# Layer 1's first head in a four-layer cross-attention kernel: its weights split in layer 0's attention, its keys formed in layer 0's FFN

## The reference

```python
# layer 0, FFN: the router picks 2 of 8 experts, but only experts 0 and 1 exist
weights = softmax(tokens @ gate_w); topk_w, topk_idx = top_k(weights, 2)
e0 = silu(x @ w0.T + b0); e1 = silu(x @ w1.T + b1)
out = e0 * fw[:, 0:1] * (fidx[:, 0:1] == 0) + e1 * fw[:, 1:2] * (fidx[:, 1:2] == 1)
# layer 1, attention: 8 heads of 128 over all 896 tokens and all 3000 keys
qh, kh, vh = split_heads(x @ Wq), split_heads(context @ Wk), split_heads(context @ Wv)
sim = einsum('hid,hjd->hij', qh, kh) * SCALE; mean = sim.mean(-1, keepdims=True)
attn = softmax((sim - mean) * 1.5 + mean)
out = merge_heads(einsum('hij,hjd->hid', attn, vh)) @ Wout + bout
# layer 1, FFN: weights rounded to -1, 0, 1 times their mean absolute value
scale = 1.0 / clip(mean(abs(w)), 1e-05); wq = clip(round(w * scale), -1, 1) / scale
```

## Time and profile before

| | |
|---|---|
| median of three executions | 1935.88 us |
| the profiled execution, its own time | 1937.66 us |
| its span from first to last instruction | 1935.7 us |
| TensorE busy, products | 1793.0 us, 93% |
| VectorE busy | 1410.4 us, 73% |
| ScalarE busy | 1020.4 us, 53% |
| GpSimd busy | 507.4 us, 26% |

### The profile page before, as it was taken

The page is one execution under the profiler, slowest core; times in us unless marked ns, Lnnn a source line. Parts: engine busy times, 40 slices in busy tenths (PEclk is TensorE's granted clock), DMA queues, the critical chain, the costliest instruction groups (busy, mean ns, idle before and its releaser), DMA issues. The chain is left out here.

```text
span 1935.7 us, 33792 instructions
## 1 busy us (share of the span) xinstructions
PE 1793.0 (93%) x11747; PEld 1585.4 (82%) x11750; DVE 1410.4 (73%) x3157; ACT 1020.4 (53%) x2247; POOL 507.4 (26%) x531
## 2 busy tenths in 40 slices
PE   7958999999999999999967999999969999999698
PEld 6637999999898989899845888888857888888587
DVE  6478787777777787778666566666777777777786
ACT  4344656555556555565535565556622666666421
POOL 0514030211203030302011233333441444343342
PEclk9978999999999999999988999999989999999799
DMA  4011000000000000000021112110000000000011
GB/s 160 1 77 33 2 4 9 2 10 0 11 0 11 0 12 0 3 0 1 1 98 49 53 58 64 47 64 14 9 1 17 15 9 23 9 10 4 23 56 40
DMA packets 17591, 48.43 MB, mean 25 GB/s; under 512 B 2602, under 2 KB 7347, under 8 KB 15796
## 3 DMA queue, kind: packets, MB, share of 16 engines
q1 hardware_dynamic: 16596, 45.99, 7.3%
q10 hardware_dynamic: 864, 0.83, 0.1%
HBM read 45.89 MB, written 0.92 MB: 24 GB/s over the span
## 5 line engine op out<-in xcount | busy, mean ns | idle before, releaser
L1280 ACT ACTIVATE a_pH<-banks 125x512 fp32r<-125x512 f32 (+1 forms) x384 | 203.9, 544 | 273.6 <-PE banks L195 192.2
L1351 DVE TENSOR_TENSOR a_pL<-banks,a_pH 125x512 fp32r<-125x512 f32 (+1 forms) x384 | 235.2, 623 | 100.3 <-ACT a_pH L1280 96.6
L1854 POOL TENSOR_TENSOR a_prob<-a_prob,a_rinv 112x750 f32<-112x750 f32 x128 | 184.1, 1438 | 395.9 <-DVE a_rinv L2157 395.9
L1327 DVE TENSOR_SCALAR_CACHE_REDUCE a_prob<-banks 128x500 f32<-128x500 f32 x336 | 223.1, 677 | 18.0 <-PE banks L195 9.0
L1181 PE MATMUL banks<-ident,a_prob 128*125 128x128 f32 x1344 | 201.6, 274 | 6.6 <-ACT a_prob L1265 4.4
L195 PE MATMUL banks<-a_pH,a_head_vH 125*128 125x256 f32 (+1 forms) x576 | 203.2, 353 | 2.1 <-DVE a_pL L1351 1.1
L1265 ACT ACTIVATE a_prob<-a_prob,a_nmax 128x1000 f32<-128x1000 f32 x168 | 188.0, 1122 | 28.2 <-DVE a_nmax L1330 28.2
L1181 PEld LDWEIGHTS banks<-ident,a_prob 128*125 128x125 f32 x1344 | 187.1, 188 | 10.0 <-ACT a_prob L1265 4.9
L1137 POOL TENSOR_TENSOR a_head_oH<-a_o,ones 128x256 fp32r<-128x256 f32 (+1 forms) x24 | 16.5, 687 | 625.5 <-DVE a_o L1360 625.5
L195 PE MATMUL banks<-a_pH,a_head_vL 125*128 125x256 f32 (+1 forms) x576 | 173.0, 300 | 0.0
L195 PE MATMUL banks<-a_pL,a_head_vH 125*128 125x256 f32 (+1 forms) x576 | 172.8, 300 | 0.0
(11 more groups left out here) (422 smaller groups left out, 5094.9 us busy)
## 6 DMA issues: line engine op xcount, KB each, us to landing
a_w_out<-in_f_out SPq DMA_DIRECT2D x6, 1024.0 KB, 4.8
...
```

Of the source, the lines that this page charges most:

```text
L1280: act.activation(pH[:, c % RING, 0:wide], TB[c % 4][0:KB, 0:wide], ACT.Copy).then_inc(t_high, 1)
L1327: dve.tensor_scalar(prob[:, at, c * CHUNK:(c + 1) * CHUNK], SB[c % 3][:, 0:CHUNK], SCALE, None, ALU.mult, ALU.max, accum_out=chunk_max[:, ...
L1351: dve.tensor_tensor(pL[:, c % RING, 0:wide], TB[c % 4][0:KB, 0:wide], pH[:, c % RING, 0:wide].bitcast(F32), ALU.subtract).then_inc(t_done, 1)
L1854: pool.tensor_tensor(both, both, rinv[:, n % RING, :].unsqueeze(2).to_broadcast([SEQ, 2, KEYS]), ALU.mult).then_inc(p_normed, 1)
```

## The change

Nine things are done in one change.

1. `PairWeights` is allocated ahead of layer 0, and layer 1's heads use its buffers. One buffer `raw` holds the pair's raw weights, or a head's (`head_raw`), or layer 0's key and value weights, which lie there first.
2. In layer 0's attention SyncE loads head 0's weights of layer 1 into it once layer 0's have been split, and GpSimd splits them (`first_head_cut`) after the context.
3. Keys of layer 1's head 0 (`s.kH`, `s.kL`) are formed in layer 0's FFN, in banks 0 to 2: chunks 0 to 2 on TensorE at the start of the phase, chunks 3 to 5 behind tiles 3 to 5 of the expert loop.
4. In that FFN GpSimd waits until x is normed before it splits the expert weights; the high part is formed by ScalarE, ahead of the turn of x. The first of the three `quant_raw` loads moves ahead of the expert weights, and its sum of absolute values ahead of the turn.
5. The other two sums stand behind the SiLUs of tiles 0 and 2. `QUANT_AT` goes from 2 to 3; the last rounding and all three conversions stand behind the loop.
6. The bias comes as 128 rows of which only rows 0 and 64 are not zero; the high part fills rows 0 to 63 and the low part rows 64 to 127, and one product with a square of ones adds both. It is 256 KB then.
7. Expert tile 0 is formed between the router's products and the transposes of the logits.
8. In layer 1 head 0 begins with four units of values, then transposes, queries, scores of tiles 0 and 1, then the other eight units. The first query waits for the bank of value unit 0, the second for that of unit 1. GpSimd adds the bias to x ahead of splitting the output weights, and head 1's weights are loaded at the start.
9. The helpers are cut up so that one unit can be issued by itself (`value_unit`, `query_half`, `key_terms`, `high_value_unit`, `sum_value_unit`, `low_query_half`). In the loop over heads they issue the same instructions as before, but the low part of the queries is a subtraction without a factor of 1.0.

```diff
-        wkv = sb("a0_wkv", [P, 2, 2, D])
+        wkv = s.pair.raw[:].rearrange("p (w k d) -> p w k d", w=2, k=2)
...
+            sp.wait_ge(w_cut, 1)
+            sp.dma_start(s.pair.head_raw, dram["a1_w"][0]).then_inc(head_loaded, 16)
...
+            pool.wait_ge(cut_done, 3 * PIECES)
+            first_head_cut(pool, s.pair, head_loaded, head_high, head_cut)
...
+    if between is not None:
+        between()
...
-        QUANT_AT = 2
+        QUANT_AT = 3
+        KEYS_AHEAD = 3
+        KEYS_BEHIND = (3, 4, 5)
+        ABS_BEHIND = (0, 2)
...
-        one = sb("f0_one", [1, P], F32R)
+        bias = sb("f0_bias", [P, WIDE])
+        bias_both = sb("f0_bias_both", [P, WIDE], F32R)
+        one = sb("f0_one", [P, P], F32R)
...
-        EB = B[4:8]
+        EB = [B[6], B[7], B[4], B[5]]
+        KEY_BANKS = B[0:3]
...
+            sp.dma_start(quant_raw[:, 0, :], dram["f1_w"][:, 0, :]).then_inc(quant_loaded[0], 16)
-            sp.dma_start(bias[:], dram["f0_bias"]).then_inc(w_loaded, 16)
-            for m in range(3):
+            sp.dma_start(bias[:], dram["f0_bias"]).then_inc(bias_loaded, 16)
+            for m in range(1, 3):
...
-            pool.tensor_copy(one[:], s.ones[0:1, :])
-            pool.wait_ge(w_loaded, 32)
-            pool.tensor_copy(biasH[:], bias[:]).then_inc(bias_high, 1)
-            pool.tensor_copy(wH[:], w_raw[:]).then_inc(w_cut, 1)
+            pool.tensor_copy(one[:], s.ones[:])
+            pool.wait_ge(ql.normed, TILES)
+            pool.wait_ge(w_high, 1)
+            pool.tensor_tensor(wL[:], w_raw[:], wH[:].bitcast(F32), ALU.subtract).then_inc(w_cut, 1)
+            pool.wait_ge(bias_loaded, 16)
+            pool.tensor_copy(bias_both[:], bias[:]).then_inc(bias_high, 1)
             pool.wait_ge(bias_high, 1)
-            pool.tensor_tensor(biasL[:], bias[:], biasH[:].bitcast(F32), ALU.subtract)
-            pool.wait_ge(w_cut, 1)
-            pool.tensor_tensor(wL[:], w_raw[:], wH[:].bitcast(F32), ALU.subtract).then_inc(w_cut, 1)
+            pool.tensor_tensor(bias_both[P // 2:P, :], bias[P // 2:P, :], bias_both[P // 2:P, :].bitcast(F32),
+                               ALU.subtract).then_inc(bias_cut, 1)
...
+            def key_low(c):
+                dve.wait_ge(k_high, c + 1)
+                dve.tensor_tensor(s.kL[:, key_cols(c)], KEY_BANKS[c % 3][:, 0:CHUNK], s.kH[:, key_cols(c)].bitcast(F32),
+                                  ALU.subtract).then_inc(k_low, 1)
...
+            for c in range(KEYS_AHEAD):
+                key_low(c)
+            at = router_exps(dve, r, q, B[3])
...
+                if i in KEYS_BEHIND:
+                    key_low(KEYS_AHEAD + KEYS_BEHIND.index(i))
+            for m in range(TILES - QUANT_AT - 2, 3):
+                quant_round(dve, m)
...
+            load_table(act, s, ACT.Sqrt)
+            key_high(0)
             layer_norm_scalar(act, ln, ql)
+            abs_sums(0)
+            act.wait_ge(w_loaded, 16)
+            act.activation(wH[:], w_raw[:], ACT.Copy).then_inc(w_high, 1)
             turn_scalar(act, ql, B[4:8], s.xnTH)
+            for c in range(1, KEYS_AHEAD):
+                key_high(c)
             router_scalar(act, r, q, B[4:8])
...
-                if i < 3:
-                    act.wait_ge(quant_loaded[i], 16)
-                    need(act, abs_summed, i)
-                    act.activation(abs_out[:], quant_raw[:, i, :], ACT.Abs, accum_out=abs_sum[:, i:i + 1]).then_inc(abs_summed, 1)
                 act.wait_ge(e_filled, i + 1)
                 need(act, x_added, i - POST + 1)
                 act.activation(post[:, i % POST, :], EB[i % 4][:, :], ACT.Silu).then_inc(post_ready, 1)
-                if i >= QUANT_AT + 3:
-                    brought_back(i - QUANT_AT - 3)
-            for m in range(TILES - QUANT_AT - 3, 3):
+                if i in ABS_BEHIND:
+                    abs_sums(1 + ABS_BEHIND.index(i))
+                if i in KEYS_BEHIND:
+                    key_high(KEYS_AHEAD + KEYS_BEHIND.index(i))
+            for m in range(3):
...
-            turn_and_route(pe, s, ql, xn, B[4:8], r, q, B[0])
+            def keys(c):
+                need(pe, k_low, c - 2)
+                split_products(pe, KEY_BANKS[c % 3][:, 0:CHUNK], key_terms(s.pair.wH, s.pair.wL, s, c)).then_inc(k_filled, 1)
+
+            def expert(i):
                 tok = slice(i * P, (i + 1) * P)
                 need(pe, post_ready, i - 3)
                 split_products(pe, EB[i % 4][:, :], [
                     pair for k in range(KT) for pair in (
                         (s.xnTH[:, k, tok], wH[:, k, :]), (s.xnTH[:, k, tok], wL[:, k, :]),
-                        (s.xnTL[:, k, tok], wH[:, k, :]))]
-                    + [(one[:], biasH[:]), (one[:], biasL[:])]).then_inc(e_filled, 1)
+                        (s.xnTL[:, k, tok], wH[:, k, :]))], True, False)
+                if i == 0:
+                    pe.wait_ge(bias_cut, 1)
+                pe.matmul(EB[i % 4][:, :], one[:], bias_both[:], start=False, stop=True).then_inc(e_filled, 1)
+
+            def first_expert():
+                pe.wait_ge(w_cut, 1)
+                expert(0)
+
+            for c in range(KEYS_AHEAD):
+                keys(c)
+            turn_and_route(pe, s, ql, xn, B[4:8], r, q, B[3], first_expert)
+            for i in range(1, TILES):
+                if i == QUANT_AT + 2:
+                    pe.wait_ge(abs_summed, 3)
+                    pe.wait_ge(q.step, 1)
+                    pe.matmul(B[3][:, 0:3], s.ones[:], abs_sum[:], start=True, stop=True).then_inc(abs_total, 1)
+                expert(i)
+                if i in KEYS_BEHIND:
+                    keys(KEYS_AHEAD + KEYS_BEHIND.index(i))
...
+        self.w_raw, self.wH, self.wL, self.wv = s.pair.head_raw, s.pair.wH, s.pair.wL, s.pair.head_wv
+        self.kH, self.kL = s.kH, s.kL
...
-    sp.dma_start(w.w_raw[:], dram_w[0]).then_inc(q.loaded, 16)
     sp.dma_start(w.wo_raw[:], dram_wo[0]).then_inc(q.wo_loaded, 16)
-    with sp.Fori(1, HEADS) as h:
-        sp.wait_ge(q.wv_cut, h)
-        sp.wait_ge(q.qk_cut, h)
+    sp.dma_start(w.w_raw[:], dram_w[1]).then_inc(q.loaded, 16)
+    sp.wait_ge(q.wo_cut, 1)
+    sp.dma_start(w.wo_raw[:], dram_wo[1]).then_inc(q.wo_loaded, 16)
+    with sp.Fori(2, HEADS) as h:
+        sp.wait_ge(q.wv_cut, h - 1)
+        sp.wait_ge(q.qk_cut, h - 1)
...
+def first_head_cut(pool, w, loaded, high, cut):
+
+    pool.wait_ge(loaded, 16)
+    pool.tensor_copy(w.wH[:], w.head_raw[:, 0:4, :]).then_inc(high, 1)
+    pool.tensor_copy(w.head_wv[:, :, 0, :], w.head_raw[:, 4:6, :]).then_inc(high, 1)
+    pool.wait_ge(high, 2)
+    pool.tensor_tensor(w.wL[:], w.head_raw[:, 0:4, :], w.wH[:].bitcast(F32), ALU.subtract).then_inc(cut, 1)
+    pool.tensor_tensor(w.head_wv[:, :, 1, :], w.head_raw[:, 4:6, :], w.head_wv[:, :, 0, :].bitcast(F32),
+                       ALU.subtract).then_inc(cut, 1)
...
-            return 0 if isinstance(h, int) and h == 0 else EACH * h - GROUPS
+            return EACH * h - GROUPS - CHUNKS
+
+        FIRST_FILLED = [("v", 0), ("v", 1), ("v", 2), ("v", 3), ("q", 0), ("q", 1)] + [("v", n) for n in range(4, VUSES)]
+        FIRST_DONE = [("v", 0), ("v", 1), ("q", 0), ("q", 1)] + [("v", n) for n in range(2, VUSES)]
+        first_filled = {each: n + 1 for n, each in enumerate(FIRST_FILLED)}
+        first_done = {each: n + 1 for n, each in enumerate(FIRST_DONE)}
+        first_bank = {each: TB[n % 4] for n, each in enumerate(FIRST_FILLED)}
+        last_in_bank = {each: FIRST_FILLED[n - 4] for n, each in enumerate(FIRST_FILLED) if n >= 4}
...
-            cut_qk(pool, s, w, q, 0, 0)
-            cut_wv(pool, s, w, q, 0, 0)
+            add_bias(pool, s, q, ql, bias)
             cut_wo(pool, s, w, q, 0, 0)
-            add_bias(pool, s, q, ql, bias)
...
-            project_keys(pe, s, w, q, GB, 0, 0, range(2))
+            def first_values(n):
+                if ("v", n) in last_in_bank:
+                    pe.wait_ge(q.done, first_done[last_in_bank["v", n]])
+                value_unit(pe, s, w, first_bank["v", n], n).then_inc(q.filled, 1)
+
+            def first_queries(n):
+                pe.wait_ge(ql.done, GROUPS // 2 * (n + 1))
+                pe.wait_ge(q.done, first_done[last_in_bank["q", n]])
+                query_half(pe, s, w, first_bank["q", n], HALVES[n]).then_inc(q.filled, 1)
+
+            for n in range(4):
+                first_values(n)
             turn_tensor(pe, ql, xn, LNB, s.ident[:])
-            project_keys(pe, s, w, q, GB, 0, 0, range(2, CHUNKS))
+            first_queries(0)
+            first_queries(1)
             pe.wait_ge(ql.done, GROUPS)
-            project_queries(pe, s, w, q, GB, 0)
-            pe.wait_ge(q.done, HIGHS)
+            pe.wait_ge(q.done, first_done["q", 0])
             scores(0, 0)
+            pe.wait_ge(q.done, first_done["q", 1])
             scores(0, 1)
-            project_values(pe, s, w, q, GB, 0, 0)
+            for n in range(4, VUSES):
+                first_values(n)
...
```

(26 more changed lines are left out.)

173 lines of the change are left out of this document (94 added, 79 removed).

## The result

The changed kernel takes 1923.79 us, the median of six executions (1921.93 to 1928.3); six of the kernel before on the same chip have a median of 1935.56. The ratio is 0.9945 with a 95% interval of 0.9932 to 0.9958: faster by 0.55%, 10.6 us, give or take 2.5 (the two medians as they stand are 11.8 apart). The forecast was 1926.4, a gain of 9.5.

What follows compares the result with a forecast made beforehand. The seam of layer 0's FFN and layer 1's attention start, where TensorE idles at a lowered clock, was taken as the place to win: +0.3 - 0.3 - 8.1 - 1.4 = -9.5 us, so 1926.4 us, range 1922.5 to 1930.5.

Steps and rivals of the forecast that it cites:

- predicted +0.3: Layer 0's attention: four moved GpSimd instructions delay one VectorE normalisation, +0.3 us.
- the rule of the Trainium skill: Layer 0's attention: a normalisation could stand behind a whole 1.2 us split, twice; +2.1 instead of +0.3, kernel at 1928.2.
- bound of 3.6: Layer 0's attention: the moved GpSimd instructions take at most 3.6 us, the upper bound on their cost.
- FFN to the turn: Layer 0's FFN: ScalarE turns x from 111.4 instead of 113.7, 2.3 us left of the norm's 4.4.
- Both branches: Router in layer 0's FFN: logits near 117.8 at 2.4 GHz, near 120.5 at 1.2 GHz; FFN -1.6 or +1.1 us.
- forecast of -0.3: Whole of layer 0's FFN: 0.3 us shorter, taken between -1.6 and +1.1 us.
- Coefficients to the FFN's end: Layer 0's FFN, VectorE: 14.3 us plus 1.8 for key splits, less 1.6 of waiting, plus 0.4 for the total: 14.9.
- first score T+13.0: Layer 1, from its start T: first score at T+13.0, between T+12.4 and T+14.3, against T+21.1; -8.1 us.
- -1.4 predicted: Layer 1, first score to first turn: VectorE has 6 sums instead of 8, GpSimd 10 splits instead of 12; -1.4 us.
- Rival 4: Layer 1: TensorE stays at 1.2 GHz until the first turn, costing 17 us, kernel at 1943; chance 0.04.
- A shift as a whole: Beyond layer 1's first turn: the stretch shifts as a whole, no duration in the head loop changes.
- the FFN's +2.3: Layer 0's FFN: only 2.3 of 4.4 us won reach the turn; +2.3 on the sum if x is turned as before.

Runs made afterwards that it cites:

- filled: Changed kernel with twelve throwaway TensorE products between the transposes of x and the router in layer 0's FFN; ratio 0.9942 to the kernel before.
- logits_first: Changed kernel with expert tile 0 behind the transposes of the logits instead of ahead of them; ratio 0.9958 to the kernel before.
- two_units: Changed kernel with two value units instead of four ahead of layer 1's queries, which get banks of their own; 1926.58 us, ratio 0.9953.
- changed_again: The changed kernel unaltered, run again beside other kernels on the same chip; 1926.42 us, ratio 0.9956 to the kernel before.
- no_hold: Changed kernel without GpSimd's wait for the normed x in layer 0's FFN; 1922.99 us in one execution.
- still_only: Kernel before, with GpSimd waiting in layer 0's FFN until x is normed, all else as before; 1929.06 us, ratio 0.9975.
- weights_only: Kernel before, with only head 0's layer 1 weights loaded and split in layer 0's attention; ratio 0.9973.
- still_and_weights: Kernel before, with GpSimd's wait in layer 0's FFN and the early split of head 0's layer 1 weights; 1926.77 us, ratio 0.9950.

## Why the prediction was right

**Layer 0.** Right in the profiled run (0.76 us in place of 0.42 for the one normalisation that fell among the four moved instructions; predicted +0.3), and it reaches the next batch: the next normalisation starts 3.33 us later, where 2.98 is the step without a hit. But the rule of the Trainium skill that I set against it, from "SBUF — State Buffer", section "SBUF: two separate sides", fits the rows better than my reading did. The changed kernel's timeline in layer 0's attention, GpSimd and VectorE:

```profile
80.39 0.61 POOL L937 CAST pair_wH<-pair_raw 128x512 fp32r<-128x512 f32 x1
...
80.45 0.76 DVE L379 TENSOR_SCALAR a_prob<-a_prob,a_rinv 112x375 f32<-112x375 f32 x1
```

and that of filled:

```profile
78.83 1.24 POOL L312 TENSOR_TENSOR ctxT<-a_raw_tail,a_tail_high 64x500 fp32r<-64x500 f32 x1
...
78.89 1.39 DVE L379 TENSOR_SCALAR a_prob<-a_prob,a_rinv 112x375 f32<-112x375 f32 x1
```

Both began 0.06 us after a GpSimd instruction and ended 0.21 us after it did: 0.76 us behind one of 0.61, 1.39 behind one of 1.24. Alone it takes 0.42. It did not end before GpSimd's instruction had, however long that was, as the rule says. The 0.36 us over the median in the earlier trace rows was no limit, only where the start happened to fall; in logits_first it fell into the moved split (1.12 us). My bound of 3.6 covered this, my value was luck within 0.7 us.

**FFN to the turn.** Right: the turn was put 8.4 us after the phase's start and came at 8.41, the norm at 2.36. The forecast that ScalarE would give back half of the norm's gain holds.

**The clock.** I left open whether it falls before the router, and priced both: logits 14.8 us after the start if it holds, 17.5 if it falls. The runs show 14.17 with it held all through (two_units), 16.72 with it low from the middle of 112 to 113, before the router's first product (changed_again), and 15.99 for the profile after, where it fell when the router had begun. Both branches were 0.6 to 0.8 too long. The forecast of -0.3 was a value between the two, and the profiled run came out there because its clock fell in between: the chip does both, with the same instructions in the same order, so that this term came so close was in part luck. The page "TensorE: Matmul & The Clock Gate" of the Trainium skill, section "HAM oscillation — how this bites in real kernels", blames waits between bursts of products. The trace agrees for the changed kernel (3.17 us of idling, then the fall); filled, where the clock fell 1.8 us into TensorE's work behind a gap of 1.48, speaks against reading it off the last gap alone. The gaps ahead of the router were 2.87 us in two_units, which kept the clock, and 3.00 and 3.17 in changed_again and after, which lost it; but in the kernel before it fell inside 138 to 139 after 2.8 us, so the length of the gap does not sort them. The prediction's 3.1 us for the fall at 104.9 was misread: TensorE's last product ended at 101.4, VectorE's last addition at 101.8, so it was 3.4.

**Coefficients to the FFN's end.** Predicted 14.9 us from the end of the coefficients to the end of round 1, 0.6 more than before; measured 14.6 (123.17 to 137.80, the first of the last two roundings), 0.3 more than before. The terms were less right than their sum. VectorE does not wait for SiLU in this loop any more, so all 2.4 us of waiting went and not 1.6; the three splits took 2.0 us, not 1.8; the 0.4 for the total did not come. Missing was that the seventh tile's additions (1.0 us), which ended behind round 1, now stand ahead of it. The last conversions follow as they did. The phase starts 1.3 us behind ScalarE's last instruction, not 0.9. The whole FFN: -0.5 against -0.3.

**Layer 1.** First query predicted at T+9.7, measured 9.54; first score T+13.0, measured 13.10, and 12.38 in the two runs in which the clock held, where the bound was 12.4. From there to the first turn -1.4 predicted; -1.0 with the clock's fall, -1.43 without. Rival 4 fell: the low clock took some nine products, from 153.7 to 157.1.

**Behind the first turn.** "A shift as a whole" holds for what the change does, not for two single executions: from the first turn to layer 1's FFN it took 793.44 us before and 791.00 after, and 790.75 to 794.50 in the runs of all kernels; layer 1's FFN 67.38 and 64.56, and 64.6 to 68.0 in all. The 5.2 us that the profiled spans differ by beyond the seam lie inside this scatter. So do the 1.06 ahead of it: in the kernel before the clock was at 0.50 from 71 to 74, in the profile after it was not. The direct part is 9.46 us, 9.1 with layer 0's hit taken off, and the measured gain 10.6 with an interval from 8 to 13: the sum was right and no luck in the spans is needed for it. It is one execution's value: in the other profiles of these instructions, changed_again and no_hold, the same stretch gives 9.9 and 11.0.

**What the prediction did not see** is that the FFN's +2.3 and its clock were a choice of the change, not a price of holding GpSimd still. still_only takes 36.18 us. The changed kernel's 4.7 more are: the turn 2.15 later (8.41 for 6.26), from the turn to the logits 2.1 more (7.58 for 5.47: 1.5 the clock and 0.6 expert tile 0 ahead of the transposes, by the 6.07 of two_units), 0.1 to the end of the conversions, and 0.4 at the phase's end. What it buys with that, the keys out of layer 1, is 2.6 us at the first score (13.10 for 15.66) and 1.0 to the first turn.

What stays open: why the phase's end costs 0.4 us more in most runs (1.3 us from ScalarE's last instruction to the next phase, against 0.93 in the kernel before and still_only and 0.98 in no_hold; it is not the changed loop, for weights_only and still_and_weights, which have the loop of before, show 1.28 and 1.27), and what decides between the clock's two courses in the same code.
